# A DLRM tower on one core: the hand-written orders of TensorE, VectorE, ScalarE and GpSimd, and the PSUM banks, are replaced by another set

## The reference, cut to what matters

```python
e = jnp.stack([tbl_0[ids[:, 0]], ..., tbl_39[ids[:, 39]]], axis=1)      # 512 x 40 x 32
vi = e[:, _I_IDX, :]; vj = e[:, _J_IDX, :]                              # 780 pairs
z = jnp.einsum('bke,kef,bkf->bk', vi, W, vj)                            # 512 x 780
h = jnp.concatenate([z, dense_ctx], axis=1)
h = jnp.maximum(h @ W_top1 + b_top1, 0.0)                               # 796 -> 512
h = jnp.maximum(h @ W_top2 + b_top2, 0.0)                               # 512 -> 256
y = h @ W_top3
```

## Time and profile before

| what | before |
|---|---|
| median of 3 runs | 185.73 us (185.0 to 186.6) |
| profiled execution | 185.81 us, span 184.0 us |
| TensorE busy (matmuls) | 170.3 us, 93% of the span |
| VectorE busy | 149.7 us, 81% |
| ScalarE busy | 88.7 us, 48% |
| GpSimd busy | 108.6 us, 59%, of it 98.3 us the 96 gathers |
| chain that ended last | TensorE 80%, VectorE 8%, ScalarE 7%, DMA 1% |

### The profile page before, as it was taken

How to read it: one execution, slowest core, us unless ns; L and a number is a source line. 1 busy time by engine, 2 the same in 40 slices (tenths; PEclk the granted TensorE clock), 3 DMA queues, 4 the chain that set the end, 5 groups by cost and what they waited for, 6 DMA issues and landing times.

```text
span 184.0 us, 4760 instructions
## 1 busy us (share of the span) xinstructions
PE 170.3 (93%) x2056; PEld 47.0 (26%) x2056; DVE 149.7 (81%) x144; ACT 88.7 (48%) x80; POOL 108.6 (59%) x104
## 2 busy tenths in 40 slices
PE   2999949999899998989999899999999899999993
PEld 0234414331324211222222222122222222222330
DVE  0989899999999589989897899978679999594600
ACT  4998878879499833240222633010463634210511
POOL 2777788787877787777777788787450040910000
PEclk9999999999999999999999999999999999999999
DMA  5997600000100107801000000000000000000000
GB/s 171 364 381 279 213 12 14 16 14 11 20 16 13 19 11 263 276 14 18 14 11 18 14 11 12 18 14 13 12 0 4 0 0 4 4 0 4 0 0 0
DMA packets 7068, 10.47 MB, mean 57 GB/s; under 512 B 2036, under 2 KB 4600, under 8 KB 7048
## 3 DMA queue, kind: packets, MB, share of 16 engines
q1 hardware_dynamic: 3944, 8.56, 13.0%
q0 software_dynamic: 3072, 1.58, 4.7%
q10 hardware_dynamic: 32, 0.03, 0.1%
HBM read 10.17 MB, written 0.00 MB: 55 GB/s over the span
## 4 chain that ended last, share of the span: by engine, by line
PE 80%; DVE 8%; ACT 7%; issue 2%; DMA 1%; DVEq 0%; ACTq 0%
PE ring_ps L643 21%; PE ring_ps L626 21%; PE ring_ps L652 14%; PE ring_ps L590 11%; DVE prod L333 8%; PE ring_ps L693 4%; PE ring_ps L572 3%; PE ring_ps L618 3%; ACT distance L422 2%; ACT one_hot L425 2%; PE ring_ps L603 2%; ACT copied L446 1%; DMA ids_sb<-hot_ids 1%; ACT ids L410 1%; ACT h L480 0%
## 5 line engine op out<-in xcount | busy, mean ns | idle before, releaser
L398 POOL DMA_INDIRECT rows<-table,idx x96 | 98.3, 1024 | 31.7 <-issue 28.7
L333 DVE TENSOR_TENSOR prod<-ring_ps,emb 128x1024 f32<-128x1024 f32 x76 | 90.0, 1217 | 11.3 <-PE ring_ps L626 10.7
L626 PE MATMUL ring_ps<-emb,wall 32*64 32x512 f32 x720 | 49.9, 611 | 4.4 <-DVE prod L333 1.8
L643 PE MATMUL ring_ps<-prod,consts_sb 128*32 128x512 f32 x400 | 50.0, 599 | 1.2 <-ACT copied L446 0.5
L446 ACT ACTIVATE copied<-ring_ps 128x1024 f32<-128x1024 f32 x24 | 24.2, 1024 | 40.2 <-PE ring_ps L626 32.1
L652 PE MATMUL ring_ps<-zt,w_sb 128*32 128x512 f32 x224 | 26.9, 596 | 0.5 <-ACT copied L446 0.5
L333 DVE TENSOR_TENSOR prod<-copied,emb 128x1024 f32<-128x1024 f32 x20 | 24.8, 1255 | 1.4 <-ACT copied L446 1.4
L333 POOL TENSOR_TENSOR prod<-copied,emb 128x1024 f32<-128x1024 f32 x4 | 10.1, 2532 | 20.9 <-ACT copied L446 20.9
L422 ACT ACTIVATE distance<-ids,vocab 128x2048 f16<-128x2048 f16 x10 | 20.0, 2002 | 3.3 <-PE ring_ps L590 3.0
L626 PEld LDWEIGHTS ring_ps<-emb,wall 32*64 32x64 f32 x720 | 11.1, 129 | 39.3 <-issue 19.1
L425 ACT ACTIVATE one_hot<-distance,vocab 128x2048 bf16<-128x2048 f16 x10 | 20.0, 2003 | 0.3
(11 more groups left out here) (27 smaller groups left out, 64.0 us busy)
## 6 DMA issues: line engine op xcount, KB each, us to landing
w_sb<-w SPq DMA_DIRECT2D x4, 512.0 KB, 5.4
rows<-table,idx POOLq DMA_INDIRECT x96, 2.4
table<-hot_table SPq DMA_DIRECT2D x2, 640.0 KB, 5.1
table<-hot_table SPq DMA_DIRECT2D x2, 512.0 KB, 3.8
wall<-w_pairs SPq DMA_DIRECT2D x2, 512.0 KB, 9.0
wall<-w_pairs SPq DMA_DIRECT2D x2, 384.0 KB, 7.7
wall<-w_pairs SPq DMA_DIRECT2D x1, 640.0 KB
wall<-w_pairs SPq DMA_DIRECT2D x2, 256.0 KB, 6.8
```

The source lines that it names most:

```text
L333: return eng.tensor_tensor(prod[:, o % RING_P], products, emb[:, slots:slots + 1, :].to_broadcast([P, 2, BATCH]), ALU.mult)
L398: nc.gpsimd.indirect_dma_start(rows[:, k, c, r, :], None, tables[f], bass.IndirectOffsetOnAxis(ap=idx[:, c, f:f + 1], axis=0)).then_inc(ga ...
L626: mm = nc.tensor.matmul(pair(("map", g), i // 2)[to, i % 2, :], wall[own, g, to], emb[own, stream, :], start=True, stop=True)
L643: mm = nc.tensor.matmul(bank(("z", k))[DIM * g:DIM * (g + 1), :], sel[:, m, :], prod[:, t // 2 % RING_P, t % 2, :], start=m == 0, stop=last)
```

## The change: another order on each engine

Only tables of numbers change; no instruction of another kind is added and the total of each kind of TensorE work is the same. Three of the tables in short:

```diff
-TENSOR_ORDER = ("iiillllllillllllllllmmtsllmlllmlllllsmssmsmsmtllmlssmlllmlllssmlsmsmsmsmsmtsmm1mssmssmsmtsm1mssm1mmm"
+TENSOR_ORDER = ("iilllllilllllllllllimtlmlllmllsmllsllsmsmsmstmlllmlllmlslmlsmlsmssmsmstmsmssmm1mssm1mssmtsmssmsmmm1m"
...
-POOL_OPS = [74, 85, 93, 94]
-COPIED_OPS = [25, 27, 29, 35, 36, 43, 53, 55, 56, 59, 61, 73, 76, 77, 78, 80, 83, 87, 88, 90]
-SCALAR_ONE_HOTS = [4, 10, 16, 20, 25, 26, 27, 33, 34, 35]
...
+POOL_OPS = [72, 75, 77, 80, 83, 85, 88, 91, 97]
+COPIED_OPS = [27, 31, 33, 35, 36, 39, 49, 51, 53, 54, 56, 67, 69, 70, 71, 73, 79, 82, 87, 93, 95]
+SCALAR_ONE_HOTS = [4, 20, 25, 26, 27, 28, 30, 34, 35]
```

More of the change, by code:

```diff
@@ L98 @@
 TAIL = (5, 6)
-TENSOR_ORDER = ("iiillllllillllllllllmmtsllmlllmlllllsmssmsmsmtllmlssmlllmlllssmlsmsmsmsmsmtsmm1mssmssmsmtsm1mssm1mmm"
-                "ssm1mssmtsmssmssm1mssm1m1mstmssm1mssmmsm1sms1mssms1mssm1s")
-BANKS = ("0123456701235670142345670132534670134670145670145670135346701346701734012345014523450145230164523670"
-         "1345672014567014501745673014567015236701456723501674672301237670123674012375601235670156723017562301"
-         "6750123236701457234560123601452345601234501762345")
-VECTOR_ORDER = ("rooooooooroooooooorowwwoowowowwwrwwwwwwowoowwwowowwwwwwwwwwwwwwwwwwwwwwwwwwwwwwwwwwwwwwwwwwwwwwwwwww"
-                "wawawwawwwwwwawwwwwwwawwwwawwawwwa")
-SCALAR_ORDER = ("IIIoIIIoLoLIILooLooLooozLcccLzcccL1z11ccccc1LzcccLcccczccccccz")
-POOL_OPS = [74, 85, 93, 94]
-COPIED_OPS = [25, 27, 29, 35, 36, 43, 53, 55, 56, 59, 61, 73, 76, 77, 78, 80, 83, 87, 88, 90]
-SCALAR_ONE_HOTS = [4, 10, 16, 20, 25, 26, 27, 33, 34, 35]
+TENSOR_ORDER = ("iilllllilllllllllllimtlmlllmllsmllsllsmsmsmstmlllmlllmlslmlsmlsmssmsmstmsmssmm1mssm1mssmtsmssmsmmm1m"
+                "sssmssm1mtsmssmmm1mssm1mstms1mssmssm1mmssmssm1sm1sm1sms1s")
+BANKS = ("0123456730145723014567320145670153467013467012367401234670123670123670152367012367234016723670123674"
+         "5301672456730145670154567014567450123456730145201674501734567013467014523016734501723456014562345601"
+         "4523014523601234567301456701501675670150167542013")
+VECTOR_ORDER = ("rooooooooroooooooooorowoowwowwworwwwwwwwowwowwowowwwwwwwwwwwwwwwwwwwwwwwwwwwwwwwwwwwwwwwwwwwwwwwwwww"
+                "wwawwawwawwwwwawwwwwawwawwawwa")
+SCALAR_ORDER = ("IIIIoLIILIIoLooLooLooozLcLcczccc1Lc1zcccc11LzccccccccLccccczccccccz")
+POOL_OPS = [72, 75, 77, 80, 83, 85, 88, 91, 97]
+COPIED_OPS = [27, 31, 33, 35, 36, 39, 49, 51, 53, 54, 56, 67, 69, 70, 71, 73, 79, 82, 87, 93, 95]
+SCALAR_ONE_HOTS = [4, 20, 25, 26, 27, 28, 30, 34, 35]
 def within(g):
```

## The result

The changed kernel took 189.41 us (median of 4 runs, 188.53 to 190.07), beside 186.08 for the kernel before in the same comparison (4 runs, 185.0 to 186.6): a ratio of 1.019, 95% interval 1.016 to 1.022. It is slower by 1.9%. The forecast was 186.5 and "same"; its range ended at 188.8. Run again later beside other kernels it took 188.06 (4 runs, 187.17 to 189.29), ratio 1.011 [1.006, 1.017]; that lies inside the stated range. Medians are of all runs; ratios leave out runs over 1.5% above the fastest of their kernel. The profiled execution took 188.53, the fastest of the first four runs.

The account below looks back on a forecast made before the run. TensorE's work plus idle was taken as the bound, with gathers gating turn 9 at 133.3; adding 0.6, 31.8 and 0.5 gave 166.2, then 18.5 of tail and 1.8 around it gave 186.5 us, range 184.2 to 188.8.

Parts of the forecast that it names:

- the start, to turn 4: Up to turn 4: map0,1 gains 1.5 us, lost waiting at turn 2; turn 4 at 48.3, stage loses 0.8 us.
- the sum: Whole kernel: 133.3 + 0.6 + 31.8 + 0.5 = 166.2 at the tail, plus 18.5 and 1.8: 186.5 us.
- L: Landing of quad 9's rows, predicted 133.3; time is 186.5 + (L - 133.3) as long as L is above 131.3.
- gate: At turn 9: TensorE arrives at 131.3 and waits 2.0 us for quad 9's rows, so short waits ahead cost nothing.
- A longer slow start: Rival, at the start: TensorE's early half pace lasts longer, costing half a us per us, but hidden; no chance given.
- cover of 1.0 us: At turn 4: 1.0 us there hides the slow start again if it delays VectorE's pieces too.
- TensorE's work from turn 4 to turn 9: Between turns 4 and 9: 82.0 us of work, where 84.4 us lay before.
- Behind turn 9: From turn 9 to the tail: 0.6 for the turn, 31.8 us of work, 0.5 of waits; tail starts at 166.2.
- block between GpSimd and VectorE: Rival, behind turn 9: the engines block each other, three multiplies hold sums by 0.7 us each, 188.6; chance 0.09.
- The price of a copied multiply to the gathers: Beside the gathers: each copied multiply costs 0.28 us; five more add 1.4 us, bounds 0 and 4.0.
- Short waits between turn 4 and turn 9: TensorE between turns 4 and 9: seven waits of 0.1 to 0.25 us for copies and z tile 2, 1.0 in all.
- The gathers lose more: Rival, at turn 9: quad 9 lands at 134.4 or later, slower by 1%, up to 135.9 and 189.1; chance 0.14.

Follow-up runs that it names:

- e1_fill: Changed kernel with 8 extra thrown-away matmuls ahead of turn 2, filling TensorE's wait there; 186.27 us, ratio to before 1.003.
- e5_after: The changed kernel itself run again, with no edit, beside other kernels on one chip; 188.06 us, ratio to before 1.011.
- e6_late: e1_fill plus 8 more filling matmuls (1.0 us) ahead of turn 7; 186.38 us, ratio to before 1.003.
- e3_direct: Changed kernel with the 15 copied ops below 72 multiplied by VectorE straight from PSUM, without copies; 200.14 us, ratio to before 1.066.
- e4_both: Changed kernel with 8 filling matmuls ahead of turn 2 and turn 9 two steps later on TensorE; 186.92 us, ratio to before 1.005.
- e15_push16: e1_fill plus 1.6 us of filling matmuls behind turn 2, ahead of lookup 16; 187.31 us, ratio to before 1.009.
- e2: Changed kernel with turn 9 two steps later on TensorE, behind map78,79 and sum70,71; 187.36 us, ratio to before 1.007.
- e7: Changed kernel with the third spread put back ahead of the first lookup; 187.94 us, ratio to before 1.010.
- e14: e1_fill plus 24 filling matmuls (2.9 us) behind turn 2, ahead of lookup 16; 187.41 us, ratio to before 1.009.

## Why the prediction was wrong

**The step that failed** is in the start, to turn 4: "That is a gain of 1.5 us, and it is lost at once: turn 2 comes next". The wait was foreseen in its place and length ("an idle TensorE of over 2 us ahead of turn 2": 2.34), and charged at its length alone. It was taken for lost time, which is over when it ends. It was not: the clock went to half for 6.8 us, from inside the wait on. Turn 4 came at 49.83, not 48.3, with no wait ahead of it where about 1 us was forecast. With the wait filled (e1_fill) it came at 47.54 and the kernel took 186.27.

**In the terms of the sum** the error arrives as L, the landing of quad 9: 135.50 for 133.3. The prediction's own formula, 186.5 + (L - 133.3), gives 188.7 for it, and the profiled execution took 188.53. So turn 9 was a gate in the changed kernel too, as predicted; what was wrong is that the gathers were taken to keep their own time whatever TensorE does ahead of it. The first stage was late, VectorE with it, and the gathers met other instructions of VectorE; why just those is the open part above.

The rival "A longer slow start" had the mechanism and put it in the wrong place. It priced half pace before map0,1 and found it hidden, and never asked whether a wait made by the change could bring half pace back. At turn 4 its cover of 1.0 us was to hide a delay; against e1_fill the delay was 2.3 us (49.83 for e1's 47.54), and turn 4 was reached 1.1 us behind its rows.

The Trainium skill ("TensorE: Matmul & The Clock Gate", Part 1) says that the throttled clock is the default and that activity releases it. The trace agrees as far as it goes: the level falls beside an idle stretch and comes back under work. The same page of the Trainium skill (HAM oscillation) advises, for matmuls with few rows, to do more of the work ahead of each wait for a DMA so that TensorE stays warm; the runs agree, with 188.06 of e5_after and 186.38 of e6_late on one chip.

**What held.** Map0,1 at 22.73 (23.2). TensorE's work from turn 4 to turn 9, 81.58 us (82.0). Behind turn 9, 32.6 us (0.6 + 31.8 + 0.5 = 32.9), with no block between GpSimd and VectorE that held a sum by more than that. The tail, 18.45 (18.5). With the wait at turn 2 filled, the sum comes out: 47.54, 132.03, 133.26, 166.01 for 48.3, 131.3, 133.3, 166.2, and 186.27 for 186.5. So the rest of the sum was near that of the kernel without the fall of the clock, in part by luck: turn 4 was 0.8 us sooner than predicted and the short waits behind it 1.7 us longer, which the gate hid, and two errors in L cancelled, as follows.

**What was mis-sized.** The price of a copied multiply to the gathers: 0.28 us each from the trace of before, 0.33 in e1_fill and 0.37 in the changed kernel (5.2 and 5.9 us over 16 of them), 0.42 by e3_direct. The five more were to add 1.4 us; all together they added 2.1 in e1_fill, where the rest of VectorE's work cost the gathers some 0.8 less than before, and 2.8 in the changed kernel, where it cost them 0.8 more. Short waits between turn 4 and turn 9: 84.31 - 81.58 = 2.7 us, where I found seven of 1.0 together; e1_fill has as much (84.49 - 81.76), and the gate takes it up there. The landing of quad 9: 133.3 predicted, 135.50 measured. "The gathers lose more" had that size (from 134.4 on slower by 1%) and the chance of 0.14; its reason, the new pairs of copied multiplies, does not explain the lateness by itself, since e1_fill has the same pairs and landed at 133.26. The forecast (185.6 to 187.6) held only for the kernel with the wait filled.

## What to carry to other kernels

Price a wait of TensorE by its length and by what comes behind it: look in the trace whether the granted clock falls behind waits like it, put what follows down at half pace, or fill the wait. A gate that absorbs lateness (here up to 1 us at turn 9) holds only for lateness that does not also move the transfer behind the gate; ask what the late engine does to the transfer. And a profile can be of a run 1 us or more off the median (e4_both, e15_push16): look at how its run stands among the others before reading a cause from it.

## What the runs showed of the hardware

- **2.3 to 2.5 us of idle brought TensorE from 2.4 to 1.2 GHz**, for 6.8 us in the profiles of the changed kernel (waits of 2.34 and 2.30) and e3 (2.47), and 3.4 in that of e2 (2.42). In e7 a wait of 1.50 did not, but the clock fell inside one of 1.00 that began 1.46 us behind it. In e3 it fell later too, inside a wait of 1.24 at 111.42 that followed one of 1.68 at 109.06, and just behind one of 1.24 at 137.67 that followed one of 1.67 at 135.31. Single waits of 1.73 (before, at map0,1) and of 1.44 to 1.59 (turn 9 of the changed kernel, e5, e7, e14) passed without a fall in their profiles. By the mean clock of each run it fell in 7 of 8 runs of the changed kernel, 4 of 6 of e7, 6 of 10 of e2, 44 of 95 of the kernel before, and in none of e1_fill's ten.
- **A gather begun inside a copied multiply ends 0.81 us behind the multiply's end.** In the changed kernel, timeline of GpSimd:

```profile
85.97 1.73 POOL L398 DMA_INDIRECT rows<-table,idx  x1 [0.31 <-issue]
...
123.89 1.32 POOL L398 DMA_INDIRECT rows<-table,idx  x1 [0.30 <-issue]
```

and of VectorE:

```profile
85.67 1.22 DVE L333 TENSOR_TENSOR prod<-copied,emb 128x1024 f32<-128x1024 f32 x1
...
123.17 1.23 DVE L333 TENSOR_TENSOR prod<-copied,emb 128x1024 f32<-128x1024 f32 x1
```

In the first pair 85.67 + 1.22 + 0.81 = 87.70, the end of the first gather, and 123.17 + 1.23 + 0.81 = 125.21, the end of the second. The multiply is no longer than one that meets nothing (1.22), so only the gather pays.
- **The two engines fall into step.** In the nine profiles of the table at full clock, pushed by 0 to 2.9 us, the distance between the gathers and a multiply came out near 1.0, 2.2, 3.4 or 4.7 us and nowhere between: steps of 1.25 us, the pitch of free gathers. So a delay of TensorE did not move VectorE against the gathers in proportion.
